# Small-head attentions: the row maxima go from the sync queue to the ScalarE queue, one step later

## What is computed

```python
scores = jnp.einsum('bhsk,bhtk->bhst', Q, K) / sqrt(d_k)
scores = jnp.where(causal, scores, -jnp.inf)
probs = jax.nn.softmax(scores, axis=-1)
attn = jnp.einsum('bhst,bhtk->bhsk', probs, V)
```

## Time and profile before

| what | value |
|---|---|
| median of 3 runs | 4770.1 us |
| lowest and highest | 4769.83 and 4776.0 us |
| the profiled execution's own time | 4769.88 us |
| its span (first to last instruction) | 4768.1 us |
| PE busy | 4283.0 us, 90% |
| DVE, ACT, POOL busy | 72%, 58%, 49% |
| mean granted TensorE clock | 0.950 |

### The profile page before, as it was taken

How to read it: one execution, slowest core, us unless ns; L and a number is a source line. 1 busy time by engine, 2 the same in 40 slices (tenths; PEclk the granted TensorE clock), 3 DMA queues, 4 the chain that set the end, 5 groups by cost and what they waited for, 6 DMA issues and landing times. The chain is left out here.

```text
span 4768.1 us, 129948 instructions
## 1 busy us (share of the span) xinstructions
PE 4283.0 (90%) x54312; PEld 2101.0 (44%) x54312; DVE 3412.0 (72%) x5204; ACT 2775.9 (58%) x6997; POOL 2327.6 (49%) x1448
## 2 busy tenths in 40 slices
PE   5897999999999999976879999999999999877688
PEld 2222544544454544432434444454544444433343
DVE  3773888888888888853548888888888888733463
ACT  2664666666666666642546666666666666543354
POOL 3102766666666666642006666666666666500200
PEclk8998999999999999986889999999999999988699
DMA  5212000000000000003310000000000000000320
GB/s 150 32 19 58 2 20 7 2 20 7 20 7 20 7 2 2 2 4 41 41 37 24 2 23 3 20 6 20 7 2 24 2 2 2 2 4 9 49 33 10
DMA packets 87860, 88.62 MB, mean 19 GB/s; under 512 B 36632, under 2 KB 79860, under 8 KB 83444
## 3 DMA queue, kind: packets, MB, share of 16 engines
q1 hardware_dynamic: 86420, 74.11, 7.7%
q10 hardware_dynamic: 864, 6.29, 0.3%
HBM read 44.13 MB, written 7.34 MB: 11 GB/s over the span
## 5 line engine op out<-in xcount | busy, mean ns | idle before, releaser
L422 POOL TENSOR_TENSOR ra<-ra,rb 128x1024 f32<-128x1024 f32 x384 | 924.0, 2406 | 390.9 <-DVE rb L711 388.2
L436 POOL TENSOR_TENSOR qkr<-ra,inv 128x1024 f32<-128x1024 f32 x384 | 731.3, 1904 | 607.0 <-ACT inv L663 602.0
L466 PE MATMUL ps<-wvo,xs 128*32 128x512 f32 x6144 | 821.8, 607 | 72.6 <-ACT vs L599 52.3
L500 PE MATMUL ps<-wq,xs 128*128 128x512 f32 x1536 | 749.9, 611 | 19.5 <-DMA wq<-in_L_ffn_Wqkv 18.6
L641 ACT ACTIVATE pr<-ps,neg 128x64 f32<-128x64 f32 x3072 | 669.9, 338 | 0.6 <-DVE neg L688 0.6
L599 ACT ACTIVATE vs<-ps 128x512 f32<-128x512 f32 x768 | 451.7, 588 | 321.9 <-PE ps L466 320.2
L1428 DVE TENSOR_REDUCE nm<-ps 128x1 f32<-128x512 f32 (+3 forms) x768 | 382.1, 549 | 244.7 <-PE ps L1237 243.7
L688 DVE TENSOR_REDUCE neg<-ps 128x8 f32<-128x512 f32 x384 | 264.4, 688 | 379.7 <-PE ps L522 379.7
L652 ACT ACTIVATE inv<-ssq 128x16 f32<-128x16 f32 x384 | 82.8, 216 | 678.8 <-DVE ssq L746 678.8
L500 PEld LDWEIGHTS ps<-wq,xs 128*128 128x128 f32 x1536 | 273.4, 191 | 443.9 <-issue 352.3
L522 PEld LDWEIGHTS ps<-kt,qt 64*32 64x32 f32 x24576 | 359.5, 107 | 243.8 <-issue 243.8
(11 more groups left out here) (225 smaller groups left out, 6377.1 us busy)
## 6 DMA issues: line engine op xcount, KB each, us to landing
qs<-cut SPq DMA_DIRECT2D x216, 64.0 KB
ks<-cut SPq DMA_DIRECT2D x216, 64.0 KB
wq<-in_L_ffn_Wqkv SPq DMA_DIRECT2D x12, 1024.0 KB, 5.1
wvo<-wvo_scratch SPq DMA_DIRECT2D x12, 1024.0 KB, 4.9
wvo_scratch<-pt ACTq DMA_DIRECT2D x6, 1024.0 KB, 4.1
w<-in_L_ffn_W SPq DMA_DIRECT2D x12, 341.0 KB
pt<-in_L_ffn_Wqkv SPq DMA_DIRECT2D x6, 512.0 KB, 8.4
pt<-in_L_ffn_Wo SPq DMA_DIRECT2D x6, 512.0 KB, 7.7
```

The source lines that it names most:

```text
L422: pool.tensor_tensor(ra[:, m % 2, :, :], ra[:, m % 2, :, :], rb[:, :, :], ALU.add).then_inc(sum_done.sem, 1)
L436: pool.tensor_tensor(qkr[:, m % 2, :, :].rearrange("p s (h c) -> p (s h) c", c=HD), ra[:, m % 2, :, :].rearrange("p s (h c) -> p (s h) c", ...
L466: last = pe.matmul(VP[32 * j:32 * j + 32, :], xs[:, turn % 2, v * WIN:v * WIN + WIN], wvo[:, l % 2, j, :], start=True, stop=True)
L500: last = pe.matmul(PJ[:, qk, :], xs[:, turn % 2, t * P:t * P + P], wq[:, l % 2, at:at + 512], start=True, stop=True)
```

## The change

`maxima` leaves the sync queue's loop and goes into ScalarE's, with the same wait for DVE and the same three transfers. It is issued at step 4g + 5 in place of 4g + 4, ahead of everything else that ACT does in that step. Two waits are added to it that the order of the sync queue had given: on the memset of the rows (group 0 only) and, for the first group of batches 2 and 3, on the turned scores of the batch that last used this half of `qs`. The stacks stay where they are.

```diff
             sp.wait_ge(ones_set.sem, ones_set.at(1))
             for k in range(FIRST, LAST):
-                if k % 4 == 0 and 0 <= k // 4 - 1 < ROW_GROUPS:
-                    maxima(k // 4 - 1)
                 if (b := batch_at(k, 1)) is not None:
...
+            def maxima(g):
+                b, gb_ = divmod(g, SG)
+                act.wait_ge(mcut_done.sem, mcut_done.at(6 * g + 6))
+                if g == 0:
+                    act.wait_ge(ones_set.sem, ones_set.at(1))
+                if b >= 2 and gb_ == 0:
+                    act.wait_ge(st_mm.sem, st_mm.at(NP * SH * (b - 1)))
+                for c in range(PARTS):
+                    act.dma_start(qs[M_ROW + c:M_ROW + c + 1, b % 2, 4 * gb_:4 * gb_ + 4, :].rearrange("o h (i t) -> o (h i) t", i=TB), mcut[:, g % 2, c, :]).then_inc(ld_m[g % 2].sem, 16)
+
             for k in range(FIRST, LAST):
+                if k % 4 == 1 and 0 <= k // 4 - 1 < ROW_GROUPS:
+                    maxima(k // 4 - 1)
                 if (g := group_at(k, 8)) is not None:
```

## The result

The changed kernel takes 4856.7 us (4854.5 to 4866.4), the kernel before on the same chip 4773.0 (4769.8 to 4779.6): a ratio of 1.0177, 95% interval 1.0159 to 1.0196. It is slower, as forecast, but by 84 us instead of 28, and just outside the range (4850). The profiled execution's span is 4855.9 us against 4768.1, so 87.8 us are to be explained; both lie within 4 us of their kernel's median.

What follows compares the result with a forecast made beforehand. PE, busy 90% of the span, was taken as the bound, so its waits count. Against 4769.9 us: + 96 (ACT's issues) - 71 (maxima waits) - 19 + 22 (clock) = + 28, so 4798 us, 0.6% slower; range 4750 to 4850.

Steps and rivals of the forecast that it cites:

- The pauses on ACT: Step 4g + 5: three issues ahead of the exponentials delay PE, 96 us over the 45 groups after each stage's first.
- the 8.6 us that I left as waits for ACT in the first groups: First groups of the latent and plain stages: 5.5 and 3.1 us of PE's waits stay, behind ACT's late square.
- The group of 13.5 us: An ordinary group of four steps was to take 13.5 us instead of 11.5.
- The rival with the issue at 0.33 us: ACT's step 4g + 5: issues cheap or covered, 61 us instead of 96, kernel faster at 4753; chance 0.19.
- The maxima's waits: PE's eleven waits for the row maxima in the three attentions, 79.5 us, were to go, for a gain of 71.
- The maxima still land late: Rival: maxima land at 8 us beside the stacks, six meetings keep about 3 us each, +18, 4816; chance 0.06.
- another queue lets them pass in 1.7 us: Maxima issued from ACT's queue were to land in about 1.7 us even beside the stacks.
- Net of the waits: PE's waits: 96 us added by ACT's issues against 71 us gained from the maxima.
- The clock: PE's clock: one in four of the new pauses lowers it, costing 22 us; 19 us come back from removed waits.
- 19 us given back: PE's lower-clock work behind the removed maxima waits stays at 2.4 GHz: 19 us gained, between 0 and 27.
- Between none and all (45 x 3 us = 135 us): Bounds on what the 45 pauses of PE cost through its lower clock; 22 us was taken.
- The pauses pull the clock down often: Rival: one in two pauses or more lowers PE's clock, 60 to 110 us instead of 22, about 4860; chance 0.13.

Runs made afterwards that it cites:

- run 4: The changed kernel with the maxima issued behind ScalarE's exponentials of step 4g + 5 instead of ahead of them: 4791.1 us, 1.0034 of the kernel before.
- run 7: The changed kernel with the maxima issued by GpSimd at step 4g + 4 instead of by ScalarE, stacks as before: 4765.0 us, 0.9981 of the kernel before.
- run 9: The changed kernel with the maxima behind ScalarE's exponentials of step 4g + 5 and the stacks spread as in run 5: 4794.0 us, 1.0039 of the kernel before.
- run 6: The changed kernel with the stacks spread as in run 5: 4852.4 us, 1.0166 of the kernel before.
- run 5: The kernel before with the stacks of batches 1 to 3 in four lots of 9, behind the maxima of steps 4, 8, 12 and 16: 4712.2 us, 0.987.
- run 8: As run 5, but with three lots of 12 at steps 4, 8 and 12: 4704.0 us, 0.9856 of the kernel before.
- run 1: The changed kernel with 32 small unused matmuls before turned piece 2 of the groups that pause: 4821.4 us, 1.0099 of the kernel before.
- run 1b: The kernel before with the same 32 small matmuls at the same place as in run 1: 4818.1 us, 1.0094 of the kernel before.

## Why the prediction was right in direction and wrong in size

**The pauses on ACT: right.** I took 0.587 us an issue from the sync queue's row, with no such issue of ACT to look at; it is 0.607. I took 96 us in sum, besides the 8.6 us that I left as waits for ACT in the first groups, so 104.6; the waits for ACT rose by 102.4. The group of 13.5 us is there where the clock stayed up. The rival with the issue at 0.33 us is refuted by that row.

**The maxima's waits: nearly right.** 79.5 us were to leave these waits altogether; 67.7 did. In the first latent group ACT's square is late next, as worked out, and PE waits for the exponential behind it:

```profile
2255.11 0.29 PE L1247 MATMUL ps<-ident,cmask 128*128 128x128 bf16 x1 [7.16 <-ACT pt L1391]
```

I had 5.5 us here. The 11.8 us that are left have the cause that I gave 0.06: "The maxima still land late". The assumption that another queue lets them pass in 1.7 us was wrong.
The Trainium skill, page "DMA: Bandwidth & Descriptors", section "Issuing engines are not separate DMA queues", said that a second engine saves only the time to start a transfer; runs 4, 7 and 9 and the 10.6 us above agree. What the same page of the Trainium skill, in its section "Queues, rings and completion order", has of engines that take turns between queues does not show in this trace.
The packets of the three transfers with the 10.6 us show where it sticks. Of the 16 data packets of each, half started within 1.5 us of the issue. The other half started 7 to 9 us later, while packets of the stacks ran throughout. The trace names no DMA engine for a packet. That the late half is the half on the engines that carried the stacks is inferred: a transfer of stacks comes with 8 packets of 4 bytes besides its data, one of the maxima with 16. In the step they are needed there is slack for most of that, so this error cost little in the changed kernel (11.8 us), and more in runs 4, 7 and 9 (44.6, 37.3 and 43.0 us). For run 9 I left it out again; for runs 4 and 7 I had counted late landings, for run 7 with 10 to 25 us.

**Net of the waits:** I had + 25 (96 - 71), the profile has + 31.7. This part of the sum holds.

**The clock: the step that failed.** The prediction had "I take one in four, with 2 us each: 22 us" lost behind the pauses and 19 us given back behind the waits that go, + 3 net. Measured: + 57.3 us of busy time for the same matmuls, net of what was given back, and + 67 in run 6 against run 5. The 19 may well be right in size (run 8 shows 12.2); with 12 to 19 of it the loss is 69 to 76 us. The loss was too small by a factor of about three. By its own upper end, "Between none and all (45 x 3 us = 135 us)", 67 us are one half. The rival "The pauses pull the clock down often", with 60 to 110 us and about 4860, is what happened, and I gave it 0.13.

The argument that misled me was about the rows: I asked whether the pauses are nearer to the waits of 4 to 6 us, all followed by the lower clock, or to those up to 1.6 us, of which one in six was, and leaned on the second. But those were single waits in otherwise full work, and the change makes one in every group. That it is the pauses which bring the clock down is shown by runs 1 and 1b; from what length or frequency on they do is not.

**The sum** with the measured terms: + 102.4 for ACT, - 67.7 for the maxima, about - 3 in the rest of PE's waits, + 57.3 for the clock, + 89 against 87.8.

**What stays open:** why packets of another queue start late beside a backlog; whether the maxima would land in time from another queue if they went out ahead of the spread stacks, as they do on the sync queue in runs 5 and 8 (no run has this); and how much of the busy time that runs 4 and 9 have above the kernel before (40.5 and 30.6 us) comes from the waits for the landings.

## What to carry to other kernels

A transfer issued in front of the work of an engine that feeds TensorE costs its issue time (here 0.6 us each) as soon as the idle time before it is used up, and a wait put in front of the issue uses it up: + 7 and + 17 us alone, and 140 together (run 6 against run 5), the lower clock included. Count what regular pauses do to TensorE's clock as a term of its own (here 57 us beside 102 us of waits). And where small urgent transfers are late behind bulk ones, another queue alone gained little or nothing here (0.2% at best): cut the bulk into lots and put each behind the urgent one on the same queue (here 1.4% gained instead of 1.8% lost).

## What the runs showed of the hardware that I had not expected

Pauses of about 2 us in TensorE, one in every 13 us or so of full work, were followed by half clock in many groups: 57 to 67 us of added busy time in 45 pauses, and 32 small matmuls in each took it away (busy time less filler 4278 us against 4340; with the filler in both kernels the difference is 7.1 us). A small transfer from ScalarE's or GpSimd's queue landed up to 11 us after its issue when the sync queue's bulk transfers were under way, against a median of 1.6 to 1.8, and only half of its packets were late.
